# A decoder stack on one core: new orders of all engines from another table of places

## The reference, cut to what matters

```python
x = tgt + att(tgt, memory)[0]         # L0: the attention of sequence 0 alone is used, and added to every sequence
h = mamba2_block(x, ...)              # L1: conv of 4 taps, silu, a scan over 128 tokens, a gate, a norm
x = h + cross_attention(ln(h), ctx)   #     8 heads
x1 = ln(x + mha(x, x, causal))        # L2: 16 heads; padded keys dropped
x2 = ln(x1 + mha(x1, ctx));  x = ln(x2 + mlp(x2))
a = ln(causal_attention(x, ctx) + x)  # L3: 16 heads
x = gelu(a @ W1.T + b1) @ W2.T + b2 + a
```

## Time and profile before

| | |
|---|---|
| time, median of 3 runs | 1669.34 us (1668.79 to 1673.69) |
| the profiled execution's own time | 1673.93 us |
| its span from the first to the last instruction | 1672.1 us |
| mean granted TensorE clock | 0.989 of full speed |
| TensorE busy | 1609.6 us, 96% |
| VectorE busy | 1387.7 us, 83% |
| ScalarE busy | 1073.6 us, 64% |
| GpSimd busy | 494.2 us, 30% |

### The profile page before, as it was taken

One profiled execution on the slowest core, in us unless ns is written; L12 is line 12 of the kernel. 1 busy time (PEld: TensorE's weight loads), 2 busy tenths in 40 slices (PEclk: granted clock), 3 DMA queues, 4 the chain that ended last, 5 costly groups with the idle time before them and its releaser, 6 DMA issues.

```text
span 1672.1 us, 61077 instructions
## 1 busy us (share of the span) xinstructions
PE 1609.6 (96%) x24963; PEld 1383.7 (83%) x24963; DVE 1387.7 (83%) x3587; ACT 1073.6 (64%) x2797; POOL 494.2 (30%) x1256
## 2 busy tenths in 40 slices
PE   7889999999999999999999999999999999999886
PEld 6777888888888888888888888888888888888774
DVE  4588888888888889888888988888898888888552
ACT  2356666766666676666667666666766666676552
POOL 1333223333322332332233233223323322332110
PEclk9999999999999999999999999999999999999997
DMA  6120001000000000000000000000000000000000
GB/s 208 43 81 21 5 19 31 18 25 28 21 2 25 24 25 25 25 22 4 25 24 25 24 24 23 4 24 25 25 24 25 16 10 24 22 28 18 5 5 7
DMA packets 31316, 44.36 MB, mean 27 GB/s; under 512 B 3008, under 2 KB 26176, under 8 KB 30912
## 3 DMA queue, kind: packets, MB, share of 16 engines
q1 hardware_dynamic: 31040, 40.46, 7.6%
HBM read 36.12 MB, written 4.33 MB: 24 GB/s over the span
## 4 chain that ended last, share of the span: by engine, by line
PE 56%; DVE 35%; issue 5%; POOL 2%; DMA 1%; ACT 1%; DVEq 0%; SPq 0%; POOLq 0%; ACTq 0%
PE ring L639 20%; PE ring L645 14%; PE ring L627 6%; DVE conv L1363 5%; DVE maxima_at L1261 5%; PE score L707 4%; DVE decay L1397 3%; PE score L731 3%; PE ring L773 3%; DVE conv L1369 2%; PE ring L858 2%; DVE decay L1401 2%; DVE QB L1272 2%; DVE conv L1358 2%; PE score L671 2%
## 5 line engine op out<-in xcount | busy, mean ns | idle before, releaser
L1538 POOL TENSOR_TENSOR stat<-stat 128x1 f32<-128x1 f32 x224 | 131.7, 594 | 612.8 <-DVE stat L1227 612.3
L1019 ACT COPY actT<-ring 128x256 f32<-128x256 f32 x256 | 95.5, 373 | 264.6 <-PE ring L627 264.2
L1261 DVE TENSOR_REDUCE maxima_at<-score 128x4 f32<-128x512 f32 x388 | 240.8, 684 | 26.0 <-PE score L707 25.2
L1052 ACT ACTIVATE weights<-score 128x512 f32<-128x512 f32 x388 | 200.6, 607 | 28.6 <-PE score L731 28.1
L1363 DVE SCALAR_TENSOR_TENSOR conv<-raw,vectors,conv 128x128 f32<-128x128 f32 x576 | 169.2, 349 | 6.8
L639 PE MATMUL ring<-actT,w_q 128*128 128x128 f32 x1024 | 141.4, 281 | 0.7 <-ACT actT L1019 0.7
L639 PEld LDWEIGHTS ring<-actT,w_q 128*128 128x128 f32 x1024 | 124.5, 191 | 12.8 <-issue 11.3
L639 PE MATMUL ring<-actT,w_up 128*128 128x128 f32 x1024 | 129.1, 280 | 0.5 <-ACT actT L1019 0.5
L639 PEld LDWEIGHTS ring<-actT,w_up 128*128 128x128 f32 x1024 | 120.6, 194 | 3.7 <-ACT actT L1019 1.1
L731 PE MATMUL score<-QB,KE 32*128 32x128 f32 x3104 | 116.7, 286 | 3.8 <-issue 2.8
L1187 ACT ACTIVATE gT<-ring,vectors 128x128 f32<-128x128 f32 x256 | 73.0, 368 | 70.3 <-PE ring L639 69.6
(11 more groups left out here) (179 smaller groups left out, 3809.7 us busy)
## 6 DMA issues: line engine op xcount, KB each, us to landing
decay<-rates_out SPq DMA_DIRECT2D x32, 512.0 KB, 4.1
cT<-in_ctxT SPq DMA_DIRECT2D x32, 128.0 KB, 2.2
x_in<-in_x SPq DMA_DIRECT2D x32, 128.0 KB, 2.5
out<-result SPq DMA_DIRECT2D x32, 128.0 KB, 2.1
row_all<-in_rows SPq DMA_DIRECT2D x1, 1420.0 KB, 10.2
w_in<-in_in_proj SPq DMA_DIRECT2D x1, 1288.0 KB, 6.5
w_k<-in_k SPq DMA_DIRECT2D x4, 256.0 KB, 7.4
w_v<-in_v SPq DMA_DIRECT2D x4, 256.0 KB, 7.2
```

Source lines behind the costliest of these rows:

```text
L1019: nc.scalar.copy(dst.rearrange("p c k -> p (c k)"), t[:, 0:n]).then_inc(read, 1)
L1052: run(weights[:, turned_buffer(it, a_, l), r, :], score[:, r, :], ACT.Exp).then_inc(S["exps"], 1)
L1261: nc.vector.tensor_reduce(maxima_at[:, maxima_buffer(it, a_, l), 32 * r:32 * (r + 1)].rearrange("p (f s) -> p s f", f=2)[:, 0:DC, :], scor ...
L1538: tt(stat[:, l, 10:11], stat[:, l, 2:3], stat[:, l, 4:5], ALU.pow).then_inc(S[done], 1)
```

## The change

The numbers of the tables `TASKS`, `FIRST`, `LAST`, `SETUP` and `SHIFT` are others; the code that uses them is the same, and each engine has the same instructions as before in another order. The file becomes five lines shorter, so a line of the functions has a number smaller by 5 (L1397 is L1392). A few rows of the tables:

```diff
--- before.py
+++ after.py
@@ -48,165 +48,160 @@
 TASKS = dict(
...
-    scan=14.2492, scores1=32.2004, scores2=32.0011, scores3=47.3368, scores4=68.1586, silu=20.9204, softplus=18.9875,
-    spread=22.7901, store=23.1605, turn1=32.8102, uT=26.5226, up0=66.8312, up1=67.8745, values1=33.4323, values2=42.004,
-    xbc0=16.7051, xbc1=18.0605, xhat=30.6529, xhatT=15.884, xnT=28.5927, z0=20.9215, z1=17.7244)
...
+    proj=26.3005, quads1=30.3743, quads2=37.4984, quads3=45.5767, quads4=56.9082, quadsT2=39.8474, quadsT3=48.5593,
...
+    softplus=18.1967, spread=22.1943, store=35.4371, turn1=31.9825, uT=25.7639, up0=66.0566, up1=67.1262, values1=32.5485,
...
+    x5T=55.2027, x6T=64.7087, xbc0=15.9402, xbc1=17.4311, xhat=30.6782, xhatT=15.2464, xnT=27.9389, z0=19.8459, z1=17.0546)
...
 FIRST = dict(
-    K1=(0, -4.8807, 1.8851, 0, 0, -0.0386, 0, 0.3068), K2=(0, 0, 0.0587, 0.2116, 0.4008, -0.0391, 0, 0.0921),
...
+    K1=(-3.5863, 0.014, 0.0039, 0.1437, -0.004, -0.0764, -0.0045, 0.0148),
...
 SHIFT = dict(
...
-        xnT=0.9282, z0=0.0015, z1=0.2322, K0=-24.9607, Q0=-31.7526, V0=-0.7018, attT0=-21.6729, exps0=39.9731, prep_in=-3.1006),
...
+        x3T=-0.0524, x4T=-0.0914, x5T=0.4602, x6T=0.0187, xbc0=0.0794, xbc1=0.1534, xhatT=0.1738, xnT=1.1875, z0=-0.0141,
...
-        n2=-0.0248, n3=2.0304, norm5=3.5039, proj=0.6654, softplus=1.1659, uT=-0.0221, x1r=1.4386, z0=1.9558),
...
+        n2=0.6395, n3=1.5137, norm5=3.992, proj=1.6103, softplus=0.4902, uT=0.6536, x1r=2.7112, z0=2.1025),
...
-        ld=8.6234, loadc=-5.0975, loadx=16.7863, spread=13.2176, store=78.055, load_mamba=-31.3063, load_w1=-56.8981,
...
+        ld=0.7653, load_mamba=-0.1333, load_w1=-6.4978, load_w2=3.0654, load_w3=-6.7229, loadc=-18.3276, loadx=-3.2479,
```

More of the change, by code:

```diff
@@ L50 @@
 TASKS = dict(
[L51 to L54, removed]
@@ new lines @@
+    mT3=47.724, mT4=58.206, n2=40.1873, n3=46.8406, norm2=33.4765, norm3=21.9655, norm4=36.5694, norm5=61.854, pairs=21.1037,
+    proj=26.3005, quads1=30.3743, quads2=37.4984, quads3=45.5767, quads4=56.9082, quadsT2=39.8474, quadsT3=48.5593,
+    quadsT4=61.0399, row=43.7153, scan=13.61, scores1=31.2809, scores2=30.9799, scores3=46.6315, scores4=67.5193, silu=20.2792,
+    softplus=18.1967, spread=22.1943, store=35.4371, turn1=31.9825, uT=25.7639, up0=66.0566, up1=67.1262, values1=32.5485,
+    values2=41.35, values3=49.6955, values4=62.301, x1=13.6404, x1r=11.5008, x2T=34.5477, x3T=43.8698, x4T=51.6314,
@@ L190 @@
+    load_mamba=-169.8473, load_w1=-124.6961, load_w2=-23.7124, load_w3=0.4078, mT0=-32.3707, prep_in=-5.2455,
+    prep_masks=0.1152, prep_out=1.6765, prep_q1=19.7468, quads0=-42.6316, quadsT0=-29.5486, scores0=-183.0223,
+    values0=-17.9061)
 SHIFT = dict(
     ACT=dict(
[L192 to L193 removed]
@@ L194 @@
-        fc1=0.7372, ld=-0.1039, row=0.2044, scores1=-0.7902, silu=-0.1882, softplus=-0.2365, turn1=0.1793, uT=0.4762, up0=0.6797,
-        up1=0.4246, x1=-0.5175, x2T=-0.0673, x3T=0.071, x4T=0.2522, x5T=0.318, x6T=0.3578, xbc0=0.1868, xbc1=0.439, xhatT=0.0635,
-        xnT=0.9282, z0=0.0015, z1=0.2322, K0=-24.9607, Q0=-31.7526, V0=-0.7018, attT0=-21.6729, exps0=39.9731, prep_in=-3.1006),
-    DVE=dict(
-        K1=1.0572, K3=0.57, V4=0.4841, Wo=1.1062, Y=0.609, conv0=3.1201, conv1=22.4343, decayed=-7.3402, down=1.5737, e2=0.5677,
-        e3=-0.0785, fc2=0.652, finish1=43.3665, finish2=0.278, finish3=2.0689, finish4=1.3234, mT2=0.6229, mT3=0.8259, mT4=0.5286,
-        n2=0.9079, n3=0.7485, norm2=10.4211, norm3=29.708, norm4=17.8864, norm5=2.0685, pairs=0.2116, proj=0.8909, scan=10.8396,
-        scores1=-0.5025, scores2=7.84, scores3=-0.7238, scores4=-9.0893, silu=1.0136, softplus=0.4775, uT=0.6437, x1=-1.3524,
-        x1r=1.7364, x3T=0.0339, xhat=-15.2978, xnT=0.2024, finish0=3.4964, mT0=-11.4439, prep_in=10.1597, prep_masks=14.7529,
-        prep_out=12.705, prep_q1=-0.1445, scores0=-43.4431),
+        K0=-8.3317, K2=0.2934, K4=0.2413, KE2=2.9315, KE3=-8.327, Q0=11.8487, Q1=0.2474, Q2=0.0739, Q3=0.1526, Q4=1.3768,
@@ new lines @@
+    DVE=dict(
+        K1=1.6538, K3=0.5098, V4=0.7141, Wo=0.7895, Y=0.5645, conv0=3.0128, conv1=22.5508, decayed=-7.3476, down=1.7371,
+        e2=0.3216, e3=0.1291, fc2=0.4597, finish1=43.6842, finish2=0.453, finish3=2.37, finish4=1.3421, mT0=2.6573, mT2=0.4172,
+        mT3=0.4996, mT4=0.4072, n2=0.4604, n3=0.5253, norm2=10.1134, norm3=29.8324, norm4=17.9085, norm5=2.3303, pairs=0.2301,
+        prep_in=-1.5863, prep_masks=15.9741, prep_out=15.7202, prep_q1=-2.3378, proj=1.1564, scan=11.1196, scores0=7.1965,
+        scores1=-0.3859, scores2=7.9493, scores3=-0.8869, scores4=-9.0593, silu=0.9298, softplus=0.4599, uT=0.5588, x1=-1.3919,
+        x1r=2.2935, x3T=0.0731, xhat=-16.0773, xnT=0.4225),
```

252 lines of the change are left out of this document (123 added, 129 removed).

## The result

The changed kernel took 1676.9 us in the median of nine runs (1672.6 to 1681.3), the kernel before 1669.3 on the same chip; the ratio is 1.0043 with an interval of 1.0026 to 1.0059. A second set of runs gave 1.0023 (1.0011 to 1.0036). The changed kernel's median was 1675.5 us there, the other's 1671.3. So it is slower, by 0.2 to 0.4%: both intervals leave out no change, but the difference, 4 to 8 us, is small beside the spread of single runs, 7 to 10 us in a set. The forecast was 1671 us and no measurable difference.

A forecast was written before the change was run, and what follows sets the result against it. TensorE and the turn through VectorE were taken to limit together. Steady lanes +1, ramp +1 and end 0 gave +2 us, put to the median of 1669.3: 1671 us, range 1660 to 1680.

The forecast's parts named there:

- the gate products that the prediction priced: GpSimd's products beside VectorE's silu: same slot in steady lanes, 0 to 2 us saved, taken as 0.

The follow-up runs named there:

- copies in every second lane: The changed kernel with one copy of the tiny matmul n3 added in every second lane, against the kernel before: ratio 1.0015.
- after + 24: The changed kernel with 12 copies of the tiny matmul n3 (24 instructions) added in lane 0, against the kernel before: ratio 1.0020.
- copies placed: The changed kernel with 10 copies of the tiny matmul n3 in lane 0 and one in each of 19 later lanes, against the kernel before: ratio 1.0015.
- x3T first with the copies of n3: The kernel before with x3T ahead of xbc0 in 16 lanes, 24 padding instructions in lane 0, one n3 copy in each of 16 lanes: ratio 1.0037.

## What to carry to other kernels

Read the waits for "issue" of an engine that is 96% busy and list them by task: one such wait in a trace of before says that an instruction packet can come late there, and a new order can turn one into five. The risk here was where 258 short instructions (e3, values1, n3, quadsT4) stand in under 3 us. When a task is moved within a period, ask on which side of the wait that closes the loop it lands: ahead of Y 0.2 us less work of TensorE was worth nothing, behind it 0.1 us more was paid in every lane. And take the cost of a pair of tasks from starts in the timeline, not from the pieces of the chain.

## What was not expected of the hardware

A stall of 1.5 us can cost twice: in the second trace of the changed kernel the granted clock fell to half right behind the stall of lane 13, and the period that it fell in was 51.9 us where the first trace has 50.3.

```profile
780.00:789.00 9.00, 7.77 (x170) 6.53 (x169) 8.71 (x29) 6.82 (x21) 2.49 (x11) 1.00 0.01 3
789.00:793.00 4.00, 3.70 (x33) 3.19 (x33) 2.40 (x9) 1.19 (x3) 2.86 (x14) 0.57 0.02 4
```

The clock fell behind one stall each in three other traces (copies in every second lane, after + 24, copies placed) and behind two in that of x3T first with the copies of n3, beside the falls in the end told above; behind most stalls it did not fall. And of VectorE and GpSimd it is the second that pays, in the rows below. In lane 1 of the changed kernel silu started 0.05 us ahead of the gate product and took its least, while the product took 2.04 instead of 1.28:

```profile
74.21 2.04 POOL L1573 TENSOR_TENSOR zs<-tz,zs 128x512 f32<-128x512 f32 x1
...
74.16 0.96 DVE L1364 SCALAR_TENSOR_TENSOR conv<-raw,conv 128x768 f32<-128x768 f32 x1
```

In lane 12 of the kernel before GpSimd's drop started 0.04 us ahead of silu, and silu took 1.39:

```profile
600.76 0.62 POOL L1598 TENSOR_TENSOR V<-V,keep 128x256 f32<-128x256 f32 x1 [0.31 <-ACT tz L1116]
600.80 1.39 DVE L1369 SCALAR_TENSOR_TENSOR conv<-raw,conv 128x768 f32<-128x768 f32 x1
```

The Trainium skill ("SBUF — State Buffer", "Who interferes with whom") has it that the order of issue decides who blocks; both rows agree. In lane 15, an ordinary one, the drop starts 0.33 us ahead and silu takes 1.10. Where it starts 0.6 us ahead or more, or not beside silu at all, as in the 13 lanes of the changed kernel, silu takes 0.96; the drop itself is 0.62 us long. So the 0.14 above silu's least comes from the drop of n3 ahead of it, not from the gate products that the prediction priced.
